# Mamba block, quantized MLP and mixture of experts on one core: the order of work at the hand-over between two batches

## The chip, the cores and the metric

The kernel runs on one core of one Trainium2 chip, as one launch. The metric is the device time of that launch in microseconds (us), the median of several runs. Engines are named as in the profile: PE is TensorE, DVE is VectorE, ACT is ScalarE, POOL is GpSimd, SP is SyncE, which here only issues DMAs.

## The reference

x has 4 batches of 512 tokens by 512 features. Each batch passes three layers, each with a layer norm ahead of it and added to x behind it:

- a Mamba mixer: `xi` and `z` (1024 channels each) by one projection; a causal convolution of 4 taps over xi and a silu give u; a projection of u gives dt (128), B and C (16 each); delta = softplus(dt_w dt + bias); a scan over time h = exp(delta A) h + delta u B for 1024 channels times 16 states, y = sum over the states of h C, plus u D; y silu(z), then an output projection;
- an MLP of two linears in simulated int8 (`_smooth_quant_linear`): columns of activations and weights are smoothed by their maxima, rows are scaled and rounded to integers, multiplied, and scaled back; a silu gate lies between the two, and the weights are the batch's own;
- a mixture of 16 experts, 2 for each token, and a shared expert.

## The kernel before

**Tiles and stages.** The channels lie in 8 blocks of 128 partitions, time in 512 columns. A unit is one block with one state: 128 units a batch. VectorE runs a scan and a product with C for each unit. A chunk, on GpSimd, is delta u B for two units (`chunk`, L665, one operation on 128x1024). ScalarE makes the exponentials of delta A (`decay`), and TensorE adds up the products of the states with identity matmuls.

The program is a row of stages: `first`, then for each batch b a `scan_stage(b)`. In the scan stage of batch b the experts of batch b-1 run beside the scan. Between two scan stages stands `between(a, m)` with a = m+1, the hand-over: the projections, convolution, dt, B, C and delta of batch a, woven by hand with the quantized MLP of batch m. There are three of these (a = 1, 2, 3). `last` does the MLP of the last batch alone. Every engine has its own instruction list, written out by hand in this order; they meet by semaphores only, and each engine runs strictly in its order.

**The hand-over on TensorE** (L2144 to L2193). xi and z blocks are eight matmuls each, dl (L1894) is one block of delta. The second MLP layer (layer 1) is `gated_rows` (transposes of the gated activations, L2095), `diag_rows` (broadcasts the smoothing factors along rows, L2057), `scale_rows` (the weights' scales, L2066), `integers` (transposes, L2072), and `linear` (L2086). Before the change `gated_rows` stands behind z2 and dl 1, and `linear(m, 1)` behind z6 and dl 5.

**On ScalarE** (L1136 to L1190): `gates` (L1109) is the silu of layer 0's output, `relus` (L901) gives the abs and the relu of delta's input, `exps` and `lns` the other parts of the softplus, `magic_rows` (L1082) the rounding, `weight_scales` (L1099) the copy of the scales, `row_norm` (L1091) the norm ahead of the experts. `decay` for the first three units stands behind the last z copy and ahead of the second `row_norm`.

**On VectorE** (L1580 to L1638): the class `Quant` has the MLP's steps; `one_more` and `lost` (L1276, L1288) are the softplus steps on e = exp(-|x|) of one block: w = e + 1, then e is overwritten by what the rounding of w lost. Blocks 0 to 3 stand inside layer 1's steps, blocks 4 to 7 behind `row_stats` and directly ahead of the scan.

**On GpSimd** (L699 to L716, L785 to L823): `softplus_sum` adds the logarithm to delta, `softplus_less` subtracts what was lost, then `du_block` and the chunks. The scan stage's loop runs over k, one chunk for each k; `pair` adds two products.

**Where e lies.** `sp_e` (L261) puts e of blocks 0 to 3 in `pairs` and of blocks 4 to 7 in `work[:, 4096:6144]`. The same columns of `work` are slots 2 and 3 of the four chunk slots (`dBu`, L220), so `chunk` waits for the subtractions of two blocks each before chunks 2 and 3:

```python
                if k in (2, 3) and b > 0:
                    pool.wait_ge(S["delta_ready"], NBLK * b + 2 * k + 2)
```

CB, the tile of C's rows broadcast over the partitions, has rows 12 to 15 that the MLP uses as scratch in the hand-over: `dg` (the diagonals) in rows 12 and 13, `wsc` (the copy of the scales) in row 14, `wrow` in row 15 (L235, L236, L252).

**Loads.** SyncE runs one list (L559 to L599). z's and xi's weights go through a ring of four slots (`wst`, `weight`, L398); a load waits until the block four places earlier is done. `bc_rows` writes B and C to DRAM, `broadcast(b, g)` (L436) reads four rows of B and four of C back, 1 MB each, for all partitions: group 0 once the first layer's integers are made, group 1 after the second linear, groups 2 and 3 after its residual, each with loads between them. ScalarE's queue stores the last batch's output (1 MB, L938) from a = 2 on. GpSimd's scan loop, ScalarE's x copies for the router (`x3`, L969, which wait for all eight sums because x3T holds the w of blocks 4 to 7), the logits (L1929), the router on VectorE and the first expert (L1971) follow in the first steps of the scan stage.

## Time and profile before

| | us |
|---|---|
| median of 3 runs | 1658.12 |
| lowest and highest | 1655.14, 1658.79 |
| the profiled execution, its time | 1660.13 |
| its span, first to last instruction | 1658.4 |
| its mean granted TensorE clock, of full speed | 0.937 |

The profiled execution is 2.0 us above the median; 1.7 us of its time lie outside the span. Times in the views are us from the start of the span. In a timeline several equal operations are merged into one row with their count; the bracket is the idle time of the engine ahead of the row and what ended it. Busy matmul times are modelled at their ends, so a chain of z blocks takes 3.44 us a block although a row says 3.60, and a delta block 0.86 although it says 1.02 or 1.10.

### The profile page before, as it was taken

Reading aid. Unit: us, or ns where it says so; the run is one execution under the profiler, and the core shown is the slowest. Engines: PE = TensorE matmul, PEld = TensorE weight load, DVE = VectorE, ACT = ScalarE, POOL = GpSimd, SP = SyncE. Lnnn points to the kernel's source line nnn. Section 1 sums busy time; section 2 is a strip of 40 time slices with the busy share of each in tenths; the row PEclk is TensorE's granted clock in tenths of the full one; section 3 lists DMA queues with packets and bytes.
Section 4 is the critical chain, followed back from the end, with each engine's and each line's share of the span. In section 5 each row is a group of like instructions: output and inputs, shape, how many; then the busy total and the mean of one; then the engine's idle time right before and its main releaser. Section 6 shows DMA issues by size and latency. Waiting matters only on the chain.

```text
span 1658.4 us, 19268 instructions
## 1 busy us (share of the span) xinstructions
PE 1415.7 (85%) x5374; PEld 811.2 (49%) x5382; DVE 1321.6 (80%) x2196; ACT 802.4 (48%) x1369; POOL 1033.5 (62%) x672
## 2 busy tenths in 40 slices
PE   7588678997799899998799899998699899646994
PEld 4333234443465565444465565444456564334783
DVE  4588999687899999696899999786899999774212
ACT  3675444247445765337444765347544654131131
POOL 0399899104899898303899898403999898422001
PEclk9799889999799999999799999999799999868997
DMA  3550000414346683504446673604445773601984
GB/s 120 223 190 25 1 0 31 141 32 183 134 153 217 211 246 111 187 26 177 161 146 223 213 238 104 206 26 156 182 147 183 219 240 103 240 25 43 351 327 136
DMA packets 94073, 252.13 MB, mean 152 GB/s; under 512 B 11024, under 2 KB 11152, under 8 KB 88848
## 3 DMA queue, kind: packets, MB, share of 16 engines
q1 hardware_dynamic: 86688, 229.93, 40.9%
q0 software_dynamic: 5120, 16.78, 3.0%
q10 hardware_dynamic: 2160, 4.19, 0.8%
q8 instruction: 44, 0.72, 0.2%
q14 instruction: 61, 0.50, 0.1%
HBM read 207.87 MB, written 42.99 MB: 151 GB/s over the span
## 4 chain that ended last, share of the span: by engine, by line
PE 45%; DVE 20%; issue 14%; POOL 13%; ACT 4%; DMA 3%; DVEq 0%; POOLq 0%; SPq 0%; ACTq 0%
PE bank L1991 10%; POOL work L674 6%; DVE bank L1306 5%; PE bank L1831 5%; PE bank L2117 5%; PE bank L1921 4%; PE bank L1926 4%; PE bank L2020 3%; PE bank L1915 2%; PE bank L1844 2%; PE bank L2012 2%; DVE pairs L1316 2%; PE bank L1967 2%; DVE work L1316 1%; DMA wst<-in_w_in 1%
## 5 line engine op out<-in xcount | busy, mean ns | idle before, releaser
L674 POOL TENSOR_TENSOR work<-du,BB 128x1024 f32<-128x1024 f32 x255 | 599.1, 2357 | 5.4 <-DVE work L1577 3.5
L962 ACT ACTIVATE bank<-delta,A_sb 128x512 f32<-128x512 f32 x512 | 349.2, 690 | 450.7 <-DVE pairs L1316 242.3
L1306 DVE TENSOR_TENSOR_SCAN bank<-bank,work 128x512 f32<-128x512 f32 x432 | 522.0, 1220 | 27.3 <-POOL work L674 21.1
L1991 PEld LDWEIGHTS bank<-x3T,ew_up 128*128 128x128 f32 x1488 | 217.9, 193 | 73.7 <-issue 63.7
L1991 PE MATMUL bank<-x3T,ew_up 128*128 128x128 f32 (+1 forms) x1488 | 239.7, 306 | 2.2 <-issue 2.2
L1316 DVE TENSOR_TENSOR pairs<-bank,CB 128x512 f32<-128x512 f32 x240 | 161.7, 674 | 4.7 <-PE bank L1926 2.9
L1921 PE MATMUL bank<-pairs,ident 128*128 128x512 f32 x160 | 90.4, 649 | 47.0 <-POOL pairs L727 18.4
L1316 DVE TENSOR_TENSOR work<-bank,CB 128x512 f32<-128x512 f32 x192 | 128.9, 671 | 0.0
L624 POOL TENSOR_TENSOR col<-col,halfpow 128x4 f32<-128x4 f32 (+1 forms) x8 | 7.3, 912 | 191.4 <-DVE col L1454 191.4
L1844 PE MATMUL bank<-xT,wst 128*128 128x512 f32 x256 | 120.4, 617 | 4.6 <-DMA wst<-in_w_in 4.6
L2117 PE MATMUL bank<-wst,zg 128*128 128x512 f32 x256 | 117.0, 593 | 0.8 <-DVE zg L1326 0.8
L1831 PE MATMUL bank<-xT,wst 128*128 128x512 f32 x256 | 114.4, 593 | 0.7 <-ACT xT L843 0.7
L1333 DVE SCALAR_TENSOR_TENSOR etm<-etm,bank 128x128 f32<-128x128 f32 (+1 forms) x124 | 38.8, 313 | 85.8 <-ACT etm L1019 85.8
L1270 DVE SCALAR_TENSOR_TENSOR u<-etm,cw,u 128x512 f32<-128x512 f32 x96 | 71.9, 752 | 34.3 <-ACT u L863 31.9
L1921 PE MATMUL bank<-work,ident 128*128 128x512 f32 x160 | 85.2, 615 | 13.5 <-POOL work L727 10.0
L1926 PE MATMUL bank<-pairs,ident 128*128 128x512 f32 x160 | 89.0, 640 | 0.0
L727 POOL TENSOR_TENSOR work<-work,CB 128x512 f32<-128x512 f32 x64 | 81.3, 1270 | 11.1 <-DVE work L1306 11.0
L724 POOL TENSOR_TENSOR work<-work 128x512 f32<-128x512 f32 x48 | 60.7, 1265 | 43.2 <-DVE work L1316 43.2
L2020 PE MATMUL bank<-ew_dn,etm 128*128 128x512 f32 x138 | 72.2, 605 | 17.6 <-ACT x3T L1033 17.2
L1926 PE MATMUL bank<-work,ident 128*128 128x512 f32 x160 | 83.0, 600 | 0.0
L1844 PEld LDWEIGHTS bank<-xT,wst 128*128 128x128 f32 x256 | 50.2, 199 | 65.8 <-issue 64.5
L1306 DVE TENSOR_TENSOR_SCAN work<-bank,work 128x512 f32<-128x512 f32 x64 | 77.7, 1214 | 4.6 <-ACT bank L962 2.4
(263 smaller groups left out, 2364.5 us busy)
## 6 DMA issues: line engine op xcount, KB each, us to landing
ew_up<-in_exp_w SPq DMA_DIRECT2D x93, 512.0 KB, 3.8
ew_dn<-in_exp_w SPq DMA_DIRECT2D x93, 256.0 KB, 4.3
hm<-xs_dram SPq DMA_DIRECT2D x69, 256.0 KB, 4.6
ys_dram<-x3T SPq DMA_DIRECT2D x69, 256.0 KB, 4.3
wst<-in_w_in SPq DMA_DIRECT2D x64, 256.0 KB, 2.7
BB<-bc_dram SPq DMA_DIRECT2D x16, 1024.0 KB, 7.3
CB<-bc_dram SPq DMA_DIRECT2D x16, 1024.0 KB, 9.8
wst<-in_out_w SPq DMA_DIRECT2D x32, 256.0 KB, 3.0
```

Source lines behind the costliest of these rows:

```text
L674: nc.gpsimd.tensor_tensor(dBu[:, k % CHUNK_SLOTS, :, :], du[:, j % 2:j % 2 + 1, :].broadcast_to([P, 2, T]), BB[:, n0:n0 + 2, :], ALU.mult) ...
L727: nc.gpsimd.tensor_tensor(hi, hi, CB[:, (2 * m + 1) % NS, :], ALU.mult).then_inc(S["pool_prod"], 1)
L962: nc.scalar.activation(R[q % RING][:, :], delta[:, j, :], ACT.Exp, scale=A_sb[:, j, n:n + 1]).then_inc(S["da_ready"], 1)
L1306: V.tensor_tensor_scan(prod[c % (2 * PAIR_SLOTS)] if on_pool(q) else R[q % RING][:, :], R[q % RING][:, :], dBu[:, c // 2 % CHUNK_SLOTS, c ...
L1316: V.tensor_tensor(prod[c % (2 * PAIR_SLOTS)], R[q % RING][:, :], CB[:, n, :], ALU.mult).then_inc(S["prod_done"], 1)
L1831: ins = mm(ps[:, :], wst[:, slot, k * P:(k + 1) * P], xT[:, k, :], start=(k == 0), stop=(k == KD - 1))
L1844: ins = mm(z_bank(a, m)[:, :], wst[:, slot, k * P:(k + 1) * P], xT[:, k, :], start=(k == 0), stop=(k == KD - 1))
L1921: mm(Y[:, :], ident[:], prod[2 * (m % PAIR_SLOTS)], start=(m % (NS // 2) == 0), stop=False)
L1926: mm(Y[:, :], ident[:], prod[2 * (m % PAIR_SLOTS) + 1], start=False, stop=(m % (NS // 2) == NS // 2 - 1)).then_inc(S["nsum_done"], 1)
L1991: ins = mm(gu_bank(v)[:, part * n:(part + 1) * n], w[:, part * D + k * P:part * D + (k + 1) * P], rhs, start=(k == 0), stop=(k == KD - 1))
L2020: mm(down_ps[1][:, :], eT[:, v % 2, 0:P], w, start=True, stop=True).then_inc(S["down_done"], 1)
L2117: ins = mm(acc[t][:, :], zg[:, k, t * P:(t + 1) * P], wst[:, W_POS["o", m, k] % W_RING, :], start=(k == 0), stop=(k == NBLK - 1))
```

## The change

- `sp_e`: e of blocks 4 to 7 lies in CB rows 13, 15, 12 and 14 instead of `work`. ScalarE's abs of these blocks gets waits until the diagonals, the scales and the second layer's scaling are done with these rows.
- C rows 12 to 15 are broadcast last, on a semaphore of their own (`c_last`), when all subtractions are done and the first expert loads are issued; what reads C's last four rows waits for that. GpSimd's chunks wait only for B's rows of group 3.
- Chunks 2 and 3 lose their wait. In the loop, chunk 2 stands ahead of the four sums of blocks 4 to 7 and chunk 3 ahead of their four subtractions.
- SyncE loads z weights 4 and 5 ahead of B and C's way through DRAM.
- ScalarE: `gates` ahead of block 0's abs and relu; the roundings, the scale copy and block 4's abs and relu each moved up.
- VectorE: `one_more` and `lost` of blocks 0 to 3 are spread one by one over layer 1's steps.
- TensorE: `gated_rows` directly behind dl 0, the diagonals behind z2, the scales and integers behind z4 and dl 3, the second linear behind dl 4; z5, z6 and dl 5 follow it.

```diff
-            return pairs[:, m, :] if m < 4 else work[:, 4096 + (m - 4) * T:4096 + (m - 3) * T]
+            return pairs[:, m, :] if m < 4 else CB[:, (13, 15, 12, 14)[m - 4], :]
...
+        def b_rows_in(eng, b, n):
+            eng.wait_ge(bcast[n // 4], (16 if n >= 12 else 32) * (b + 1))
+
+        def c_rows_in(eng, b, n):
+            if n >= 12:
+                eng.wait_ge(S["c_last"], 16 * (b + 1))
+            else:
+                eng.wait_ge(bcast[n // 4], 32 * (b + 1))
...
+            def broadcast(b, g, half):
+
+                dst, landed = ((BB, bcast[g]), (CB, S["c_last"] if g == 3 else bcast[g]))[half]
+                if b > 0 and g == 3 and half == 1:
+                    sp.wait_ge(S["delta_ready"], NBLK * (b + 1))
...
                 weights("z", b, 0, 4)
+                if b > 0:
+                    weights("z", b, 4, 6)
                 bc_rows(b)
 
                 if b > 0:
                     wait(sp, "q_ready", 4 * TT * (b - 1) + 2 * TT)
-                    broadcast(b, 0)
-                    weights("z", b, 4, NBLK)
+                    broadcasts(b, 0)
+                    weights("z", b, 6, NBLK)
                     wait(sp, "lin_ps", 2 * TT * b)
-                    broadcast(b, 1)
+                    broadcasts(b, 1)
                     weights("o", b, 0, 4)
                     wait(sp, "linkO", 3 * TT * b)
-                    broadcast(b, 2)
-                    broadcast(b, 3)
+                    broadcasts(b, 2)
+                    broadcast(b, 3, 0)
                     load_first_experts(b - 1)
+                    broadcast(b, 3, 1)
                     load_experts(b - 1)
...
-                if k in (2, 3) and b > 0:
-                    pool.wait_ge(S["delta_ready"], NBLK * b + 2 * k + 2)
...
+                        if k > (1 if b > 0 else 0):
+                            chunk(b, k)
                         if k == 2 and b > 0:
                             for i in range(4, 8):
                                 softplus_sum(b, i)
-                            for i in range(4, 6):
-                                softplus_less(b, i)
-                        if k > (1 if b > 0 else 0):
-                            chunk(b, k)
-                        if k == 2 and b > 0:
-                            for i in range(6, 8):
+                        if k == 3 and b > 0:
+                            for i in range(4, 8):
                                 softplus_less(b, i)
...
+                    elif m == 4:
+                        sc.wait_ge(S["sbc_ps"], 2 * (2 * a - 1) + 1)
+                    elif m == 6:
+                        sc.wait_ge(S["wsc_ps"], 2 * a)
+                    elif m == 7:
+                        sc.wait_ge(S["linkO"], 3 * TT * (a - 1) + 2 * TT)
...
+                gates(m)
                 relus(a, range(0, 1))
-                gates(m)
...
                 exps(a, range(1, 2))
+                magic_rows(m, 1, 0)
                 z(a, 3)
                 relus(a, range(2, 3))
                 exps(a, range(2, 3))
-                magic_rows(m, 1, 0)
+                magic_rows(m, 1, 1)
                 z(a, 4)
                 relus(a, range(3, 4))
+                weight_scales(m, 1)
                 exps(a, range(3, 4))
-                magic_rows(m, 1, 1)
                 lns(a, range(4))
-                weight_scales(m, 1)
+                relus(a, range(4, 5))
                 z(a, 5)
-                relus(a, range(4, 5))
+                relus(a, range(5, 6))
                 z(a, 6)
-                relus(a, range(5, 8))
+                relus(a, range(6, 8))
...
-                for i in range(2):
-                    one_more(a, i)
-                    lost(a, i)
+                one_more(a, 0)
+                lost(a, 0)
                 q1.scale(0)
                 q1.maxima(0)
+                one_more(a, 1)
+                lost(a, 1)
                 q1.scale(1)
                 q1.maxima(1)
                 q1.weight_diag()
-                for i in range(2, 4):
-                    one_more(a, i)
                 q1.integers(0)
-                for i in range(2, 4):
-                    lost(a, i)
+                one_more(a, 2)
+                lost(a, 2)
                 q1.integers(1)
+                one_more(a, 3)
+                lost(a, 3)
...
                 dl(a, 0)
+                gated_rows(m)
                 z(a, 2)
+                diag_rows(m, 1, 0)
+                diag_rows(m, 1, 1)
                 dl(a, 1)
-                gated_rows(m)
                 z(a, 3)
                 dl(a, 2)
-                diag_rows(m, 1, 0)
-                diag_rows(m, 1, 1)
                 z(a, 4)
                 dl(a, 3)
-                z(a, 5)
-                dl(a, 4)
                 scale_rows(m, 1)
-                z(a, 6)
                 integers(m, 1, 0)
                 integers(m, 1, 1)
+                dl(a, 4)
+                linear(m, 1)
+                z(a, 5)
                 dl(a, 5)
-                linear(m, 1)
+                z(a, 6)
                 dl(a, 6)
                 dl(a, 7)
                 z(a, 7)
```

## Rows read from the trace of the kernel before

**Rows 1.** The page, busy us, share of the span, instructions.

```profile
PE 1415.7 (85%) x5374; PEld 811.2 (49%) x5382; DVE 1321.6 (80%) x2196; ACT 802.4 (48%) x1369; POOL 1033.5 (62%) x672
```

**Rows 2.** Windows: length; busy PE, PEld, DVE, ACT, POOL; granted clock; DMA share; GB/s.

```profile
420.00:440.00 20.00, 12.67 (x31) 6.19 (x32) 13.59 (x17) 9.55 (x17) 19.66 (x13) 0.66 0.32 127
...
560.00:580.00 20.00, 19.25 (x99) 12.80 (x97) 19.98 (x31) 14.47 (x27) 20.00 (x12) 1.00 0.76 224
```

**Rows 3.** Timeline of TensorE, second hand-over: start, us, operation, [idle before <-releaser].

```profile
746.71 1.10 PE L1902 MATMUL bank<-hm,dtw 128*128 128x512 f32 x2 [0.76 <-ACT hm L894]
...
760.31 5.37 PE L1844 MATMUL bank<-xT,wst 128*128 128x512 f32 x8 [2.15 <-DMA wst<-in_w_in]
...
777.21 1.67 PE L2091 MATMUL bank<-CB 128*128 128x512 bf16 x7 [0.25 <-DVE CB L1514]
...
780.44 3.60 PE L1844 MATMUL bank<-xT,wst 128*128 128x512 f32 x8
...
800.23 6.33 PE L1932 MATMUL bank<-x3T,gatew 128*17 128x512 f32 x8 [7.03 <-ACT x3T L980]
...
808.73 5.41 PE L1991 MATMUL bank<-x3T,ew_up 128*128 128x256 f32 x16
```

**Rows 4.** Timeline of VectorE, the same stretch.

```profile
753.01 1.29 DVE L1450 TENSOR_REDUCE col<-bank 128x1 f32<-128x512 f32 x2 [2.13 <-PE bank L2099]
...
756.71 0.42 DVE L1286 TENSOR_SCALAR work<-pairs 128x512 f32<-128x512 f32 x1
...
788.88 2.73 DVE L1294 SCALAR_TENSOR_TENSOR work<-x3T,work 128x512 f32<-128x512 f32 x1
...
792.59 2.34 DVE L1306 TENSOR_TENSOR_SCAN bank<-bank,work 128x512 f32<-128x512 f32 x2
...
803.56 1.23 DVE L1306 TENSOR_TENSOR_SCAN bank<-bank,work 128x512 f32<-128x512 f32 x1 [4.62 <-POOL work L674]
...
826.31 0.67 DVE L1316 TENSOR_TENSOR work<-bank,CB 128x512 f32<-128x512 f32 x1
```

**Rows 5.** Timeline of GpSimd, the same stretch.

```profile
788.52 2.54 POOL L674 TENSOR_TENSOR work<-du,BB 128x1024 f32<-128x1024 f32 x1
...
793.56 4.94 POOL L645 TENSOR_TENSOR delta<-delta,x3T 128x512 f32<-128x512 f32 x4 [2.50 <-ACT x3T L936]
...
809.60 2.35 POOL L674 TENSOR_TENSOR work<-du,BB 128x1024 f32<-128x1024 f32 x1
```

**Rows 6.** The chain that ended last, the same stretch: start, us, what.

```profile
749.12 11.06 DMA wst<-in_w_in
```

**Rows 7.** Timeline of ScalarE, the same stretch.

```profile
749.00 1.33 ACT L1112 ACTIVATE BB<-BB 128x256 f32<-128x256 f32 x4
...
788.60 2.94 ACT L1096 ACTIVATE xn<-x,row_shift,rstd 128x512 f32<-128x512 f32 x4 [0.41 <-POOL row_shift L636]
```

**Rows 8.** Timeline and window of VectorE alone: reciprocal of the weights; length, busy us.

```profile
765.06 0.18 DVE L1495 RECIPROCAL rr<-rr 128x4 f32<-128x4 f32 x1
...
756.71:771.65 14.94, 12.60 (x41) 0.89 0.26 101
```

**Rows 9.** SyncE's issues of B and C rows: us to landing.

```profile
DMA to landing us min/median/max: 4.2/8.9/18.8
```

**Rows 10.** Timeline of TensorE, third hand-over.

```profile
1183.85 5.41 PE L1991 MATMUL bank<-x3T,ew_up 128*128 128x256 f32 x16
```

**Rows 11.** Timelines of TensorE, ScalarE and GpSimd, first hand-over.

```profile
373.84 1.10 PE L1902 MATMUL bank<-hm,dtw 128*128 128x512 f32 x2 [0.76 <-ACT hm L894]
...
413.67 2.93 ACT L1096 ACTIVATE xn<-x,row_shift,rstd 128x512 f32<-128x512 f32 x4 [1.58 <-POOL row_shift L636]
...
433.79 5.34 PE L1991 MATMUL bank<-x3T,ew_up 128*128 128x256 f32 x16
...
434.66 2.35 POOL L674 TENSOR_TENSOR work<-du,BB 128x1024 f32<-128x1024 f32 x1
```

**Rows 12.** Window of TensorE: length, busy us, granted clock, DMA share, GB/s.

```profile
762.00:764.00 2.00, 2.00 (x4) 0.50 0.00 0
```

More of the change, by code:

```diff
@@ L328, in build @@
             "xi_ps xpad_ready conv_done u_ready z_ps z_ready bc_ps tok_ps tok_ready bc_ready bc_out dt_ps dt_ready dl_ps "
-            "sp_abs sp_exp relu_ready sp_w_ready sp_ln_ready sp_lost sum_ready z_silu delta_ready "
+            "sp_abs sp_exp relu_ready sp_w_ready sp_ln_ready sp_lost sum_ready z_silu c_last delta_ready "
             "a_shift_ready "
@@ L434, in bc_rows, with broadcasts @@
                 sp.wait_ge(S["bc_out"], 16 * b + 16)
-            def broadcast(b, g):
-                for half, dst in enumerate((BB, CB)):
-                    rows = bc_dram[half * NS + 4 * g:half * NS + 4 * g + 4, :]
-                    sp.dma_start(dst[:, 4 * g:4 * g + 4, :],
-                                 rows.rearrange("n t -> (n t)").partition_broadcast(P)
-                                 .rearrange("p (n t) -> p n t", n=4)).then_inc(bcast[g], 16)
+            def broadcast(b, g, half):
+                dst, landed = ((BB, bcast[g]), (CB, S["c_last"] if g == 3 else bcast[g]))[half]
+                if b > 0 and g == 3 and half == 1:
+                    sp.wait_ge(S["delta_ready"], NBLK * (b + 1))
+                rows = bc_dram[half * NS + 4 * g:half * NS + 4 * g + 4, :]
+                sp.dma_start(dst[:, 4 * g:4 * g + 4, :],
+                             rows.rearrange("n t -> (n t)").partition_broadcast(P)
+                             .rearrange("p (n t) -> p n t", n=4)).then_inc(landed, 16)
+            def broadcasts(b, g):
+                for half in range(2):
+                    broadcast(b, g, half)
             def expert(be, w):
@@ L580, in _ @@
                     for g in range(4):
-                        broadcast(b, g)
+                        broadcasts(b, g)
                     weights("z", b, 4, NBLK)
@@ L1311, in product @@
                     ve.wait_ge(S["scan_done"], q + 1)
-                    ve.wait_ge(bcast[n // 4], 32 * (b + 1))
+                    c_rows_in(ve, b, n)
                     wait(ve, "nsum_done", PAIRS * b + c // 2 - PAIR_SLOTS + 1)
```

4 lines of the change are left out of this document (2 added, 2 removed).

## The prediction

> **What bounds it now.** On the page TensorE is busy 85% of the span [rows 1], so the first question is where it is not. The busy time by 20 us shows it: well inside a scan stage (560 to 580) TensorE, VectorE and GpSimd are all busy 19 us or more of 20, while at the hand-over into that stage (420 to 440) TensorE has 12.7 us and a granted clock of 0.66, and VectorE 13.6 [rows 2]. There are three such hand-overs (a = 1, 2, 3), some 375 us apart; the change touches nothing else. I read the second, engine by engine, in the timelines.
>
> TensorE first [rows 3]. It stands 2.15 us for the DMA of z's block-4 weights, and that block then takes 5.37 us instead of 3.60: together 3.9 us. After its last z block it has nothing to do but the transposes of x, and starts the router's logits at 800.23 and the first expert at 808.73. VectorE [rows 4] waits 2.13 us for the gated rows' transposes, stands again ahead of the transposed integers, and waits 4.62 us in the scan for GpSimd. GpSimd [rows 5] is what VectorE waits for: chunk 1 at 788.52, then a hole, four sums at 793.56, then the subtractions mixed with chunks 2 and 3, because these chunks overwrite the e of blocks 4 to 7; chunk 4 ends at 809.60+2.35 = 811.95. The chain of waits agrees: DMA, TensorE, VectorE's second layer, the last softplus blocks, GpSimd.
>
> **The change, step by step (second hand-over, us).**
> 1. *z weights 4 and 5 earlier.* Now they are issued behind 2 MB of B and C rows, and z4's load takes 11.06 us [rows 6]. Ahead of those, with SyncE idle anyway, they are in long before use: the 2.15 and the 1.77 us of slow clock go. z6 and z7 stay behind the rows; they are needed 20 us after their issue, against those 11: no cost. The rows themselves leave at the same time.
> 2. *Gates before the block-0 softplus on ScalarE, gated rows before z2 on TensorE.* The gates start at 749.00 [rows 7] behind two operations of 0.68; now near 746.5. TensorE has the first delta block done at 747.65 [rows 3], idles some 0.6 us and ends the transposes at 748.6; the reduction starts at 748.7 instead of 753.01 [rows 4], 4.3 earlier. From there to the end of the diagonals are 3.7 us: 752.4.
> 3. *TensorE up to the second linear.* From 752.4: second row broadcast 0.5, two z blocks of 3.44, three delta blocks of 0.86, gives 762.4. VectorE has 12.6 us of work between the diagonals and the end of the integers [rows 8], the same instructions in another order, so it could be at 765.0. Later is ScalarE: the reciprocals of the weights' maxima come 8.5 us behind the diagonals as before (765.06+0.18 against 756.71 [rows 4, 8]), at 760.9; rounding, four operations, 2.1, 763.0; then z4's copy, abs and relu of block 3, the scale copy and the exponential, five operations on 128x512 of 0.5 to 0.6 net: 765.8. VectorE's one_more and lost of block 3 now stand ahead of both transposed copies, so these wait for that exponential: 1.1 plus 1.3 us, linear at 768.2. Before: 777.21 [rows 3], so 9.0 us earlier.
> 4. *What is late next.* z5, block 5, z6 (7.7 us) now follow the linear. It ends at 769.8, so blocks 6 and 7 start at 777.6 instead of 778.7: only 1.1 of the 9.0 us is left. From there ScalarE takes 9.5 us (abs and relu, table load, four exponentials, z7, three decays) to the row normalization at 788.60 less 0.41 of wait [rows 7]: 787.1. VectorE, early by 9, stands idle some 5 us before the exponentials of blocks 4 to 7.
> 5. *e in CB's last rows, chunks 2 and 3 ahead of the subtractions.* From row normalization to the first sum are 4.96 us [rows 5, 7]: 792.1. Chunk 2 falls into the hole before it, at no cost. Then four sums 4.94, chunk 3 2.35, four subtractions of the same length, a pair (one such operation, 1.25), chunk 4 2.35: 808.0 instead of 811.95, 3.95 earlier.
> 6. *VectorE's start of the scan.* One `lost` took 2.73 us instead of 0.69: it ran beside chunk 1 and ended 0.55 us behind it [rows 4, 5]. Now two chunks lie beside these operations instead of one, so I let two of them wait: from 783 the eight operations end at 791.0, against 792.59. Without any such wait it would be 787. The logits start 7.6 us behind the scan (800.23 against 792.59 [rows 3, 4]), because ScalarE's x copies stand behind a decay that waits for VectorE's third product: 798.6, one us later than the sums allow. Then 6.33 us, and 1.1 for a copy and the small transposes: first expert at 806.0 instead of 808.73, 2.7 earlier.
> The Trainium skill, GPSIMD Engine Reference, section Specifications, says that GpSimd's SBUF interfaces are shared with VectorE and contend with its instructions that have two SBUF inputs. The trace agrees: `lost` has two, and the scan's products, with one input in a bank, do not stretch. By that rule chunk 2 is not free: the sum without it would have the first expert 2 us earlier, and the 791.0 is the value with it.
> 7. *C rows 12 to 15 last.* They leave when the subtractions end, 804.4. A landing took 4.2 to 18.8 us, median 8.9 [rows 9]: 809 to 823. The product of unit 12 starts at 826.31 [rows 4], then near 823. Hidden. The waits that relu 4, 6 and 7 get are for things 5 us or more older. SyncE's wait in front of the third up weight holds nothing: that load waits for the first expert, at 806 plus.
>
> **Sum.** TensorE is 2.7 and GpSimd 3.95 us earlier, and the stage behind is bound by both: 3.3. The third hand-over is the same (first expert at 1183.85 [rows 10], 0.3 later in the pattern): 3.6. The first [rows 11] has no DMA wait. Its first delta block is at 373.84, so shifted by 372.9 us the row normalization would come at 414.2 against 413.67, later; first expert 433.1 against 433.79, chunk 4 at 435.1 against 437.01: 1.3. Together 8.2.
>
> One cost is open: TensorE's clock. Around the linear it stands 1.6 us for the scales, works 1.3, stands 1.6 again. A stand of 2.15 us brought the granted clock to 0.50 (1.2 GHz, the lower of its two levels) at 762 [rows 3, 12] and cost 1.77; one of 0.76 (ahead of 746.71 [rows 3]) left it at full speed. So between 0 and 1.8 us for each hand-over; two stands of 1.6 lie about as near the one as the other, so 0.9 for each: 2.7. The forecast is 8.2 - 2.7 = 5.5 us, from the profiled 1660.13 to 1654.6, and from the median of 1658.12, which is 2.0 lower, to 1652.6.
>
> **Rivals.**
> *More comes through.* All of VectorE's 4.6 and 1.4 us of waits in the early scan go, and the router is not last. For it: GpSimd, not TensorE, feeds the scan there. Against: the normalization still waits for z7's side. It gives 4 to 6 us for each, 12 to 18, some 1643. Chance 0.11.
> *Nothing measurable.* The tail of step 4 runs at the slow clock in all three, and `lost` waits for three GpSimd operations: 1.8 us later in each and another us from the port: 8.2 - 5.4 - 2 = 0.8, about 1657. For it: the first hand-over has no margin. Chance 0.20. 0.2% is 3.3 us, about what a measurement of this kernel can tell from no change.
> *Slower: the tail.* The same mechanism, one step more: TensorE has stood before the gated rows too (0.76 and 0.6 us), and if the clock is down from there, z2 ends 1.8 later, the diagonals and linear 1.4, and z5 with the next slow stretch 1.8: 3.2 against margins of 0.7, 2.7 and 3.0, and GpSimd beside it. It decides from a linear later than 770.9 in the second hand-over (2.7 us past my 768.2); at 773 in all three it costs 3 to 6 us: 1661 to 1664. Against: the idle of 0.76 ahead of the first delta block [rows 3] is followed by z blocks at full speed in all three hand-overs. Chance 0.14.
> *The C rows late* would need a landing of over 18 us on an empty queue: under 0.01. That the change does not do what it says is out for step 1, since the two loads have no other wait.
>
> **Numbers.** The forecast's own case (3.3 to 12 us faster) has 0.55; its range is 1646.5 to 1654.8. With the rivals: faster 0.66, same 0.20, slower 0.14. Leaving out most of the fast rival and half of the slow one, the range is 1646.5 to 1661.
>
> **What would show it.** Right: no DMA wait ahead of z4 and 3.6 us for it; gated rows' transposes ahead of z2; the linear near 768 in the pattern; VectorE idle some 5 us ahead of one_more of block 4; chunk 2 ahead of the sums; the scan's wait of 4.6 gone; the first expert 1, 3 and 3 us earlier. Wrong: a z5 of over 5 us at a clock of 0.50 in all three; a row normalization later than before in the second; a product waiting for C rows; or a scan stage that gives the start back, its length then more than before by the same us.

## The result and the profile after

The changed kernel takes 1648.43 us (median of 4 runs, 1647.67 to 1649.87) against 1658.45 us for the kernel before (4 runs): ratio 0.9934, 95% interval 0.9911 to 0.9956. It is 10.0 us faster; forecast were 5.5 us, with a range of 1646.5 to 1661. Its profiled execution took 1648.9 us, span 1647.2 us, which is 11.2 us less than the span of before (1658.4).

The page of the changed kernel (busy us, share of the span; for a line also count, mean ns, and the idle time ahead of it). The second and the third line are the scan on VectorE and the matmuls of the z blocks on TensorE.

```profile
PE 1411.3 (86%) x5382; PEld 809.1 (49%) x5382; DVE 1327.2 (81%) x2196; ACT 802.4 (49%) x1369; POOL 1033.4 (63%) x672
...
L1328 DVE TENSOR_TENSOR_SCAN bank<-bank,work 128x512 f32<-128x512 f32 x432 | 522.3, 1221 | 13.7 <-POOL work L691 7.4
...
L1867 PE MATMUL bank<-xT,wst 128*128 128x512 f32 x256 | 116.2, 599 | 0.0
```

The same two lines of the page of the kernel before:

```profile
L1306 DVE TENSOR_TENSOR_SCAN bank<-bank,work 128x512 f32<-128x512 f32 x432 | 522.0, 1220 | 27.3 <-POOL work L674 21.1
...
L1844 PE MATMUL bank<-xT,wst 128*128 128x512 f32 x256 | 120.4, 617 | 4.6 <-DMA wst<-in_w_in 4.6
```

The work is that of [rows 1], within 6 us on every engine; what went is waiting. The idle time ahead of these scans fell from 27.3 to 13.7 us, that for GpSimd from 21.1 to 7.4, and no z block waits for a DMA any more.

Busy time in windows of the changed kernel (columns as in [rows 2]): the first hand-over, and the same piece of a scan stage.

```profile
420.00:440.00 20.00, 13.16 (x40) 6.52 (x41) 17.02 (x34) 10.67 (x19) 20.00 (x15) 0.75 0.45 162
560.00:580.00 20.00, 19.25 (x95) 12.56 (x95) 18.15 (x26) 12.97 (x24) 19.47 (x12) 1.00 0.74 223
```

VectorE has 17.0 us of 20 instead of 13.6 at the hand-over, and TensorE's granted clock is 0.75 instead of 0.66. The scan stage's window shows less on VectorE (18.2 against 20.0); its cause comes below.

TensorE's timeline at the second hand-over of the changed kernel. Its first delta block starts at 745.94, where it was 746.71 before [rows 3], so 0.77 us go off a time of before ahead of a comparison.

```profile
745.94 1.10 PE L1925 MATMUL bank<-hm,dtw 128*128 128x512 f32 x2 [0.76 <-ACT hm L909]
746.87 1.20 PE L2122 MATMUL bank<-ident,BB 128*128 128x128 f32 x8
747.91 3.60 PE L1867 MATMUL bank<-xT,wst 128*128 128x512 f32 x8
...
764.61 0.62 PE L2104 MATMUL bank<-identb,BB 128*128 128x128 bf16 x8 [1.12 <-ACT CB L1122]
765.06 1.08 PE L1925 MATMUL bank<-hm,dtw 128*128 128x512 f32 x2
767.52 1.90 PE L2114 MATMUL bank<-CB 128*128 128x512 bf16 x8 [1.38 <-DVE CB L1536]
769.26 3.60 PE L1867 MATMUL bank<-xT,wst 128*128 128x512 f32 x8
...
798.54 5.41 PE L1955 MATMUL bank<-x3T,gatew 128*17 128x512 f32 x8 [7.57 <-ACT x3T L1001]
804.62 0.42 PE L1959 MATMUL bank<-ident,hm 17*128 17x17 f32 x4 [0.67 <-ACT hm L1007]
804.97 3.72 PE L2014 MATMUL bank<-x3T,ew_up 128*128 128x256 f32 x16
808.52 1.02 PE L1938 MATMUL bank<-pairs,ident 128*128 128x512 f32 x2
```

The gated rows' transposes stand ahead of z2, the second linear starts at 767.52, and the z block behind its two stands of 1.12 and 1.38 us runs at full speed. The first expert takes 3.72 us where it took 5.41 [rows 3]. Nothing in the forecast was a price for that. Both levels of the clock are in these rows: the granted clock is 0.50 in the first 2 us of the logits (798.5 to 800.5), and full in the whole expert.

Granted clock around that expert, of the kernel before and then of the changed one (length, busy us of PE, PEld, DVE, ACT, POOL, granted clock, DMA share, GB/s):

```profile
806.00:808.00 2.00, 0.56 (x2) 0.00 (x0) 1.09 (x2) 0.97 (x3) 1.93 (x1) 1.00 0.00 0
808.00:810.00 2.00, 1.62 (x8) 1.39 (x9) 1.48 (x2) 0.32 (x1) 2.00 (x3) 0.79 0.00 0
810.00:812.00 2.00, 2.00 (x6) 1.55 (x6) 2.00 (x4) 0.69 (x1) 2.00 (x2) 0.50 0.03 8
```

```profile
802.00:804.00 2.00, 1.95 (x5) 0.28 (x3) 2.00 (x3) 0.01 (x1) 2.00 (x3) 0.95 0.00 0
804.00:806.00 2.00, 1.38 (x9) 1.25 (x10) 0.56 (x3) 2.00 (x4) 2.00 (x2) 1.00 0.78 254
```

Before, the clock came back in the logits and fell to 0.50 (1.2 GHz) again behind a stand of TensorE of 1.82 us. In the changed kernel that stand is 0.67 us, and the clock stays at 1.00 (2.4 GHz).

VectorE and GpSimd of the changed kernel, same stretch:

```profile
748.11 1.29 DVE L1472 TENSOR_REDUCE col<-bank 128x1 f32<-128x512 f32 x2 [0.53 <-PE bank L2122]
...
782.44 0.43 DVE L1308 TENSOR_SCALAR x3T<-CB 128x512 f32<-128x512 f32 x1 [5.21 <-ACT CB L941]
782.90 2.73 DVE L1316 SCALAR_TENSOR_TENSOR CB<-x3T,CB 128x512 f32<-128x512 f32 x1
785.55 2.57 DVE L1308 TENSOR_SCALAR x3T<-CB 128x512 f32<-128x512 f32 x1
...
790.89 2.34 DVE L1328 TENSOR_TENSOR_SCAN bank<-bank,work 128x512 f32<-128x512 f32 x2
...
807.11 2.35 DVE L1328 TENSOR_TENSOR_SCAN bank<-bank,work 128x512 f32<-128x512 f32 x2 [1.55 <-POOL work L691]
```

```profile
782.50 5.33 POOL L691 TENSOR_TENSOR work<-du,BB 128x1024 f32<-128x1024 f32 x2
791.32 4.93 POOL L664 TENSOR_TENSOR delta<-delta,x3T 128x512 f32<-128x512 f32 x4 [3.49 <-ACT x3T L957]
...
804.64 2.36 POOL L691 TENSOR_TENSOR work<-du,BB 128x1024 f32<-128x1024 f32 x1
```

VectorE idles 5.21 us for an exponential of ScalarE, as forecast; two of its operations, a `lost` and a one_more, are stretched beside chunks 1 and 2. The scan's wait of 4.62 us [rows 4] is now one of 1.55, for chunk 4.

To compare kernels, the table gives starts in the second hand-over in us behind the first delta block, from the timelines, and as forecast (its times less 746.71). Below, a time with a + is such a time.

| | before | forecast | changed |
|---|---|---|---|
| second linear | 30.50 | 21.5 | 21.58 |
| row normalization | 41.89 | 40.4 | 40.44 |
| scan | 45.88 | 44.3 | 44.95 |
| chunk 4 | 62.9 | 58.9 | 58.7 |
| logits | 53.52 | 51.9 | 52.60 |
| first expert (its length) | 62.02 (5.41) | 59.3 | 59.03 (3.72) |
| first state sum | 67.26 | | 62.58 |

The row of the second linear of before shows 7 of its 8 matmuls, so its real start is about 0.2 us earlier; the same holds below where the linear reads +21.8, which is the 21.58 of the changed kernel.

The last row is 2.40, 4.68 and 4.94 us earlier at the three hand-overs, together 12.0. VectorE's gated products (y times silu(z), one for each block), taken from the last one of a stage to the first of the next, are earlier by the same 2.4, 4.65 and 4.9. The sum of the three shifts of these gated products is called the hand-over gain below.

### The profile page after: what moved, and what is told of

It is laid out like the page before. It is cut to its first block, busy times and chain, and to the rows that moved or that the text cites. A ratio compares the mean times of both kernels' runs of the same rounds, so it can differ in the third digit from the quotient of the medians.

```text
span 1647.2 us, 19279 instructions
## 1 busy us (share of the span) xinstructions
PE 1411.3 (86%) x5382; PEld 809.1 (49%) x5382; DVE 1327.2 (81%) x2196; ACT 802.4 (49%) x1369; POOL 1033.4 (63%) x672
## 4 chain that ended last, share of the span: by engine, by line
PE 47%; DVE 22%; issue 12%; POOL 10%; ACT 5%; DMA 2%; DVEq 0%; SPq 0%; POOLq 0%; ACTq 0%
PE bank L2014 10%; DVE bank L1328 5%; POOL work L691 5%; PE bank L1854 5%; PE bank L2140 5%; PE bank L1944 4%; PE bank L1949 4%; PE bank L2043 4%; PE bank L1938 3%; PE bank L1867 2%; PE bank L2035 2%; PE bank L1990 2%; DVE pairs L1338 2%; DVE work L1338 1%; DVE rr L1512 1%
## 5 line engine op out<-in xcount | busy, mean ns | idle before, releaser
L1328 DVE TENSOR_TENSOR_SCAN bank<-bank,work 128x512 f32<-128x512 f32 x432 | 522.3, 1221 | 13.7 <-POOL work L691 7.4
L2014 PEld LDWEIGHTS bank<-x3T,ew_up 128*128 128x128 f32 x1488 | 218.6, 195 | 74.5 <-issue 65.7
L1867 PE MATMUL bank<-xT,wst 128*128 128x512 f32 x256 | 116.2, 599 | 0.0
L1854 PE MATMUL bank<-xT,wst 128*128 128x512 f32 x256 | 114.4, 593 | 0.7 <-ACT xT L858 0.7
L1867 PEld LDWEIGHTS bank<-xT,wst 128*128 128x128 f32 x256 | 49.3, 194 | 60.3 <-issue 58.7
```

The costliest lines, as they stand in the source:

```text
L1328: V.tensor_tensor_scan(prod[c % (2 * PAIR_SLOTS)] if on_pool(q) else R[q % RING][:, :], R[q % RING][:, :], dBu[:, c // 2 % CHUNK_SLOTS, c ...
L1854: ins = mm(ps[:, :], wst[:, slot, k * P:(k + 1) * P], xT[:, k, :], start=(k == 0), stop=(k == KD - 1))
L1867: ins = mm(z_bank(a, m)[:, :], wst[:, slot, k * P:(k + 1) * P], xT[:, k, :], start=(k == 0), stop=(k == KD - 1))
L2014: ins = mm(gu_bank(v)[:, part * n:(part + 1) * n], w[:, part * D + k * P:part * D + (k + 1) * P], rhs, start=(k == 0), stop=(k == KD - 1))
```

## The experiments

The theory after the result (A): the hand-over gain is the order's (rows, scales and the second linear earlier) together with the C part's (e in CB's last rows, so that chunks 2 and 3 need not wait: GpSimd's hole filled, chunk 4 earlier), and TensorE's first expert comes out at the higher clock. Rival B: one part alone does it, the z weights above all. The first four kernels ran on one chip, beside 31 runs of before (median 1659.05 us).

**The z weights alone** (`w_only`): the kernel before with

```diff
+                if b > 0:
+                    weights("z", b, 4, 6)
...
-                    weights("z", b, 4, NBLK)
+                    weights("z", b, 6, NBLK)
```

> The kernel before with one part of the change alone: z weights 4 and 5 loaded ahead of the B and C rows. Theory A (the gain is made of three parts, each of which only lets the next one act): the second and third hand-over then look like the first one of the kernel before, whose first expert comes 2.1 and 2.4 us earlier in the pattern, so about 4.5 us faster in all, 1654; z4 takes 3.60 us with no wait in all three. Theory B (the DMA wait with its slow clock, 3.9 and 4.2 us, was nearly all of it and passes through whole): 8 us faster, about 1650. Theory C (hidden anyway): 1658.

Measured: 1657.65 us (12 runs, one of which took 3360.13 us and is not in the ratio), ratio 0.9986 [0.9967, 1.0005]. The z wait goes, but the scan starts at +43.6 in all three hand-overs where it was +43.6, +45.9 and +46.2, so that two of them gain about 2 us; the first expert took 5.3, 3.72 and 6.74 us. The hand-over gain is 0, 3.3 and 0.8 us. The early weights alone give less than a measurement can tell: the interval leaves room for the 4.5 us of theory A, not for the 8 us of theory B, so the weights were not nearly all of it.

**The orders undone** (`order_undone`): the changed kernel with the three engines' orders of before; on TensorE

```diff
-                gated_rows(m)
                 z(a, 2)
-                diag_rows(m, 1, 0)
-                diag_rows(m, 1, 1)
                 dl(a, 1)
+                gated_rows(m)
...
-                dl(a, 4)
-                linear(m, 1)
                 z(a, 5)
...
+                linear(m, 1)
```

> The changed kernel with the orders of TensorE, ScalarE and VectorE as before (gated rows behind z2, second linear behind z6); the early z weights, e in CB's rows and chunks 2 and 3 ahead of the subtractions stay. Theory A: chunk 2 fills GpSimd's hole, so chunk 4 ends some 2.4 us earlier than in the kernel with the weights alone, but the linear stays late; about 1651 to 1653, the first expert 1 to 2 us later than in the changed kernel. Theory B: the same as the changed kernel, 1648.5.

Measured: 1656.15 us (12 runs), ratio 0.9978 [0.9958, 0.9999].

**The C part undone** (`c_undone`): the changed kernel with the e of blocks 4 to 7 in the chunks' buffers again, so that chunks 2 and 3 wait for the subtractions, and C's last rows loaded with B's:

```diff
-            return pairs[:, m, :] if m < 4 else CB[:, (13, 15, 12, 14)[m - 4], :]
+            return pairs[:, m, :] if m < 4 else work[:, 4096 + (m - 4) * T:4096 + (m - 3) * T]
...
+                if k in (2, 3) and b > 0:
+                    pool.wait_ge(S["delta_ready"], NBLK * b + 2 * k + 2)
```

> The changed kernel without the part on e and the chunks (e of blocks 4 to 7 in work, C rows with the B rows, chunks 2 and 3 behind the subtractions as before); early z weights and the new orders stay. Theory A: VectorE waits for GpSimd ahead of unit 4 again (4 to 5 us), chunk 4 ends 2.4 us later than in the changed kernel, while only one lost operation is stretched; about 1651 to 1653. Theory B: the same as the changed kernel, 1648.5.

Measured: 1657.68 us (12 runs), ratio 0.9987 [0.9966, 1.0009]. The expectations (1651 to 1653 for both) missed: a third and a fifth of the changed kernel's gain are left in the medians, where more than half was expected; the hand-over gains are 5.5 and 2.4 us of 12.0. With `w_only` these runs make a square: the hand-over gain is 4.1 us with the early weights alone (ratio 0.9986), 2.4 with the orders added (0.9987), 5.5 with the C part added (0.9978), and 12.0 with both (0.9934). Each part adds little or nothing without the other, which also excludes rival B. The timelines say why. In `order_undone` the logits start at +54.4 instead of +52.6 and the first expert at +61.3 to +61.8: the scan is late. In `c_undone` the logits start earlier than in the changed kernel (+52.0), and yet the first expert comes at +60.5 to +60.7. VectorE, ScalarE and TensorE of `c_undone`, second hand-over:

```profile
803.43 1.23 DVE L1309 TENSOR_TENSOR_SCAN bank<-bank,work 128x512 f32<-128x512 f32 x1 [4.66 <-POOL work L676]
```

```profile
805.28 0.69 ACT L964 ACTIVATE bank<-delta,A_sb 128x512 f32<-128x512 f32 x1 [3.81 <-DVE pairs L1319]
807.00 0.69 ACT L964 ACTIVATE bank<-delta,A_sb 128x512 f32<-128x512 f32 x1 [1.02 <-DVE work L1319]
807.62 0.57 ACT L988 COPY hm<-bank 17x512 f32<-17x512 f32 x1
```

```profile
808.25 0.51 PE L1940 MATMUL bank<-ident,hm 17*128 17x17 f32 x4 [2.14 <-ACT hm L988]
```

The scan waits for GpSimd; ScalarE's decays wait for the scan's products; the copy of the logits is queued behind two of them on ScalarE; TensorE stands 2.14 us for it (2.41 and 2.77 at the other two hand-overs), and its expert then takes 6.63, 5.25 or 3.72 us in the three hand-overs. With the C part there is no such wait: in every kernel that has it, above and below, TensorE's stand is 0.66 to 0.67 us and the expert takes 3.72 us at all three. So the second order and the C part are not two gains that add; the scan's start and GpSimd's chunks each hold the other's gain back.

**The z weights undone** (`w_undone`): the changed kernel with the first diff reversed.

> The changed kernel with z weights 4 and 5 behind the first B and C rows again. Theory A: z4 is now due at 757.7 in the second hand-over and waits 2 to 3 us for its weights there and in the third, with a slow clock behind it, so the linear is 4 us later in these two: 5 to 8 us slower than the changed kernel, 1654 to 1656. If VectorE's and ScalarE's own chain (the exponential of block 3) hides the wait, 1650.

Measured: 1648.24 us (8 runs), ratio 0.9929 [0.9905, 0.9952], like the changed kernel. TensorE of `w_undone`, second hand-over:

```profile
755.22 1.95 PE L1865 MATMUL bank<-xT,wst 128*128 128x512 f32 x4 [0.39 <-DMA wst<-in_w_in]
```

This view ends in the middle of the block. The wait is 0.39 us there and 1.82 at the third hand-over, and the whole z block of eight matmuls takes 3.67 us behind either, so neither is followed by a slow one. The second linear is at +21.80, +21.82 and +23.25; the hand-over gain is 2.4, 5.8 and 3.8, together 12.0. The expected 1654 to 1656 were wrong; the alternative that the expectation named, a wait hidden by the chain of VectorE and ScalarE, is what the second hand-over shows, while at the third the linear is 1.5 us late. In the new order the weights' lead is worth nothing that shows in the medians.

The next four ran on a second chip (before: 1659.52 us, 11 runs). **Chunk 2 behind the sums** (`chunk2_late`):

```diff
                     if k > (1 if b > 0 else 0) and not (k == 2 and b > 0):
                         chunk(b, k)
                     if k == 2 and b > 0:
                         for i in range(4, 8):
                             softplus_sum(b, i)
+                        chunk(b, k)
```

> The changed kernel with one thing put back: GpSimd's chunk 2 of a block stands again behind the four sums of the softplus, not ahead of them; the C rows stay in CB's last rows. Theory A (the hole of GpSimd before the sums is what the C part gives): chunk 2 beside VectorE's last softplus operations is gone, so these take about 0.7 instead of 2.6 to 2.7 us and the scan starts about 2 us earlier (+42.8 instead of +44.95 us behind the first transpose of the gated rows' stage), but chunk 4 starts at about +61.1 instead of +58.7, the scan waits some 4.7 us for chunk 3 as in the run with the C part undone, ScalarE's exponential behind it keeps the router's copy back, and the first expert comes at about +60.6: about 1656 us, ratio 0.997 to 0.999, nearly all of the gain gone. Theory B (the two stretched operations of VectorE are a real cost and the hole is worth little): the scan's earlier start comes through, about 1646 us or less, ratio at or below 0.992.

Measured: 1654.22 us (5 runs), ratio 0.9966 [0.9952, 0.998]. VectorE of `chunk2_late`, second hand-over:

```profile
783.57 2.73 DVE L1317 SCALAR_TENSOR_TENSOR CB<-x3T,CB 128x512 f32<-128x512 f32 x1
786.22 0.41 DVE L1309 TENSOR_SCALAR x3T<-CB 128x512 f32<-128x512 f32 x1
...
810.07 2.35 DVE L1329 TENSOR_TENSOR_SCAN bank<-bank,work 128x512 f32<-128x512 f32 x2 [3.39 <-POOL work L691]
```

The one_more is back at 0.41 us, and the scan starts at +42.8 instead of +44.95: chunk 2 beside VectorE costs 2.2 us, as the sum's step 6 had it. But chunk 4 starts at +61.0 instead of +58.7 and the scan waits 3.39 us for it. The first expert comes at +58.9, no later than in the changed kernel (+60.6 had been expected), and still the hand-over gain is only 7.3 us instead of 12.0. So GpSimd's chunk 4 binds beside TensorE: its 2.3 us at each of three hand-overs cost 4.7 us of the hand-over gain, and 5 us between the two ratios to the kernel before. Theory A had the binding engine right and the first expert wrong.

**Scales and normalization early** (`norm_early`): VectorE's stand of 5.21 us says what to move next. On TensorE, with ScalarE in the same order:

```diff
                 dl(a, 4)
+                dl(a, 5)
                 linear(m, 1)
                 z(a, 5)
-                dl(a, 5)
-                z(a, 6)
                 dl(a, 6)
                 dl(a, 7)
+                z(a, 6)
                 z(a, 7)
```

and on GpSimd `norm(2 * m + 1)` ahead of the sum of block 3 instead of behind it.

> The changed kernel with the softplus chain moved up once more: the inputs of the scales of blocks 5 and 7 on TensorE ahead of the second linear and of z6, the rectified blocks and exponentials of ScalarE in the same order, and GpSimd's row normalization ahead of its sum of block 3. Theory A (the chain of the scales on ScalarE and VectorE sets when the scan starts, since VectorE stood 5.21 us for an exponential): the scan and x3 start 2 to 3 us earlier at each of three hand-overs, TensorE's stand of 7.57 us ahead of the logits falls to about 5, and the time is about 1641 to 1643 us, ratio about 0.989. Theory B (chunk 4 of GpSimd and TensorE's first expert bind, not the start of the scan): the earlier start is given back at chunk 4 (the scan waited 1.55 us for it already), within 2 us of the changed kernel: 1646 to 1649 us, ratio 0.992 to 0.994.

Measured: 1640.53 us (4 runs), ratio 0.9886 [0.9869, 0.9904]. VectorE of `norm_early`:

```profile
772.17 0.69 DVE L1307 TENSOR_SCALAR x3T<-CB 128x512 f32<-128x512 f32 x1 [0.92 <-ACT CB L941]
```

The stand is 0.92 us, the scan starts at +40.8, the logits at +49.6, the first expert at +56.0, +57.0 and +55.6. The hand-over gain against before is 21.3 us.

**The clock kept up** (`warm`): the changed kernel with dummy products, 28 behind the transposes of x and, once the second residual is done, 20 behind z7:

```diff
+                    if scan:
+                        for i in range(28):
+                            mm(Y[:, 0:P], ident[:], ones[:], start=True, stop=True)
...
+                pe.wait_ge(S["linkO"], 3 * TT * (m + 1))
+                for i in range(20):
+                    mm(acc[0][:, 0:P], ident[:], ones[:], start=True, stop=True)
```

> The changed kernel with dummy products of the identity and a 128x128 tile of ones, whose results nobody reads: 20 behind z7 and 28 behind the transposes of x, in TensorE's stands of 5.0 and 7.6 us. Theory A (the granted clock of 1.2 GHz in the logits is a cost on the path): the logits take about 3.5 instead of 5.4 us, the first expert and the first state sum come about 1.5 to 2 us earlier at each of three hand-overs, about 1643 to 1645 us, ratio 0.990 to 0.992. Theory B (chunk 4 and the scan of VectorE bind there as well, 1.55 us of wait for chunk 4): the logits are shorter in the trace, but VectorE's later products come at the same time and the time is that of the changed kernel, 1647 to 1649 us, ratio 0.993 to 0.994.

Measured: 1644.08 us (6 runs), ratio 0.9911 [0.9892, 0.993]. TensorE of `warm`, first and second hand-over:

```profile
426.94 5.30 PE L1955 MATMUL bank<-x3T,gatew 128*17 128x512 f32 x8 [2.30 <-ACT x3T L1001]
...
796.40 3.61 PE L1955 MATMUL bank<-x3T,gatew 128*17 128x512 f32 x8 [2.30 <-ACT x3T L1001]
```

The stand ahead of the logits is 2.30 us at all three, and the logits took 5.30, 3.61 and 5.19 us: the clock was kept in one of three (granted clock 1.00 through its logits, 0.62 and 0.50 in the first 2 us of the others). There the first state sum is 1.8 us earlier, and 0.3 and 0.2 in the others. The hand-over gain of this profile is 14.3 us, 2.3 more than the changed kernel's. The interval overlaps that of the changed kernel, so this points to A and doesn't prove it.

**Both** (`warm_norm`), with 14 and 20 dummies:

> Both edits of the two runs before together, with 14 and 20 dummy products. If the chain of the scales and the clock of the logits are two costs one behind the other, their gains add: about 1637 to 1640 us, ratio 0.987 to 0.989. If GpSimd's chunk 4 binds behind either, it is no better than the better of the two, ratio 0.990 to 0.994.

Measured: 1642.87 us (4 runs), ratio 0.9895 [0.9878, 0.9912]: no better than `norm_early`. The stand ahead of the logits is 3.47 us, and they took 5.3, 6.35 and 4.9 us, as in `norm_early` without the dummies, so with these counts they kept no clock, and whether the two gains would add stays open.

The last four, on a third chip (before: 1658.65 us, 11 runs). **The changed kernel once more** (`changed_again`):

> The changed kernel itself once more, beside the others on one chip. Theory A (its fall of the granted clock in the scan stage, 0.70 and 0.50 where other kernels show 1.00 behind the same stands, and the 1.8 us that it costs at two of three hand-overs, is a property of this order of instructions): the two falls are there again in the trace, ratio 0.993. Theory B (it is chance from one execution to the next): the stretch between the second and fourth gated block of a stage shows 1.00, the last mixer row of TensorE comes some 2 to 4 us earlier than 1423.6 us, and the ratio is between 0.990 and 0.994.

Measured: 1648.76 us (5 runs), ratio 0.994 [0.9926, 0.9954]: the gain is there again. The hand-over gain is 12.5 us against 12.0, in the three hand-overs 0.65, 5.6 and 6.2 against 2.4, 4.65 and 4.9, so one hand-over of one profile can be off by 1.7 us while the sum holds. Where the clock falls in the scan stages is read in the next section.

**Scales early without the edit on GpSimd** (`scales_early`):

> The run with the earlier softplus chain without its edit on GpSimd: TensorE and ScalarE take the scales' blocks 5 and 7 earlier, GpSimd's row normalization stays behind its sums and differences of block 3. Theory A (ScalarE's last exponentials alone set when VectorE's second half of the softplus begins): VectorE goes on 2 to 3 us earlier, at +34 instead of +36.5 us, but the row normalization, which x3 waits for, stays at about +40.4, so that x3 and the logits come as in the changed kernel (+52.6) and chunk 2 starts as late (+36.5): about 1646 us, ratio 0.991 to 0.993. Theory B (the earlier normalization is not needed): as in the run with both, 1640.5 us, ratio 0.989.

Measured: 1640.65 us (4 runs), ratio 0.9891 [0.9876, 0.9905], and the row normalization at +38.05 as in `norm_early`. The expectation had missed that it stands behind the same exponentials on ScalarE; GpSimd's edit is worth nothing that shows. This, a swap on TensorE and ScalarE alone, is the version to keep: 8 us faster than the changed kernel on the same chip.

**The first pair sum behind chunk 4** (`norm_pair`): `norm_early` with

```diff
-                        pair(k - PAIR_BEHIND)
+                        if not (b > 0 and k == PAIR_BEHIND):
+                            if b > 0 and k == PAIR_BEHIND + 1:
+                                pair(0)
+                            pair(k - PAIR_BEHIND)
```

> The best kernel so far (scales and normalization early) with one more exchange on GpSimd: the first pair sum of a block, 1.27 us, behind chunk 4 instead of ahead of it. The scan waited 1.22 us for chunk 4 there, and TensorE reads the pair sum only after the first expert, 4 us later. Theory A (GpSimd's chunk 4 binds VectorE's scan at each of three hand-overs, and TensorE is not the bound): the wait is gone, the later products come up to 1.2 us earlier each, 1637 to 1639 us, ratio 0.987 to 0.988. Theory B (TensorE's first state sum at +59.1 to +60.5 us behind the first transpose binds): no change, 1640.5 us, ratio 0.988 to 0.990.

Measured: 1644.25 us (5 runs), ratio 0.9908 [0.9894, 0.9922]. VectorE's next product, in `norm_early` and then in `norm_pair`:

```profile
798.77 2.34 DVE L1327 TENSOR_TENSOR_SCAN bank<-bank,work 128x512 f32<-128x512 f32 x2 [1.22 <-POOL work L691]
801.67 0.69 DVE L1337 TENSOR_TENSOR pairs<-bank,CB 128x512 f32<-128x512 f32 x1 [0.56 <-PE bank L1937]
```

```profile
800.00 2.35 DVE L1330 TENSOR_TENSOR_SCAN bank<-bank,work 128x512 f32<-128x512 f32 x2
804.11 0.69 DVE L1340 TENSOR_TENSOR pairs<-bank,CB 128x512 f32<-128x512 f32 x1 [1.76 <-PE bank L1940]
```

The wait for GpSimd is gone, and the same 1.2 us stand one row on, for TensorE's first state sum, which is where it was. In that order TensorE's first expert binds. Down to the last mixer row (TensorE's last output projection of the scan stages) the profile is that of `scales_early` (1413.86 against 1413.92 us); the 4.7 us between the spans of these two profiles lie in the last stage, and the two intervals overlap.

**The best kernel without early z weights** (`norm_no_w`):

> The best kernel so far without the early z weights: the 4th and 5th pair of z weights ordered behind the B and C rows again, as before the change. In the changed kernel taking them back cost nothing measurable (0.9929 against 0.9934), since the chain of the scales hid TensorE's wait. Theory A (here this chain is shorter by some 2.4 us, so the wait of z4, 0.4 to 1.8 us there, comes through): 1 to 4 us over the three hand-overs, ratio 0.990 to 0.992. Theory B (it is hidden still): ratio 0.988 to 0.989.

Measured: 1643.78 us (6 runs), ratio 0.991 [0.9894, 0.9926]. TensorE of `norm_no_w`, third hand-over:

```profile
1121.89 5.37 PE L1864 MATMUL bank<-xT,wst 128*128 128x512 f32 x8 [2.27 <-DMA wst<-in_w_in]
```

Here the wait is there with its slow z block, as in [rows 3], and the linear comes at +25.4 instead of +21.8, the scan at +44.4 instead of +40.8. At the first two hand-overs nothing changes. The hand-over gain is 16.3 us against 21.3 of `norm_early`. In the shorter order the weights' lead is worth up to 3.6 us for one hand-over in which the load is late; the medians point the same way, with intervals that overlap.

## Why the prediction was right, and what it mis-sized

Steps 1 to 7 were made in the times of before; set against the changed trace (the table above), they hold within 0.7 us.

*Steps 2 and 3.* The reduction starts 2.17 us behind the first delta block (forecast 2.0), the linear at 21.58 (21.5), after stands of 1.12 and 1.38 us. *Step 4.* Blocks 6 and 7 at +31.05 (30.9), row normalization at +40.44 (40.4): of 8.9 us at the linear, 1.45 are left. *Step 5.* The sums at +45.4 (45.4), chunk 4 done at +61.1 (61.3). *Step 6.* The scan at +44.95, 0.65 later than forecast; two operations were stretched as the step said, by 2.0 and 2.1 us: a `lost`, which has two inputs, and a one_more, which has one and went from 0.42 to 2.57 us. The Trainium skill, GPSIMD Engine Reference, section Specifications, gives the contention for VectorE's instructions with two SBUF inputs, which the prediction quoted, and also for those in a 2-port perf mode. The trace agrees for `lost`; no run here shows in which mode the one_more ran. The first expert came within 0.3 us of the forecast by luck in part: the scan was 0.65 late, and the logits took 5.41 us instead of the 6.33 taken over from before. *Step 7.* The C rows are issued at 803.50, and no product waits for them. The first hand-over has its first expert at +59.17 (forecast 433.1 less 373.84, so 59.3).

Four terms of the sum were off.

*The clock's cost, 2.7 us, was 0.* The two stands of about 1.6 us behind each other were 1.12 and 1.38, with 1.5 us of work between, and z5 took 3.60 us at all three hand-overs.

*The first expert's length was no term.* The sum counted its start (2.7 us for the second) and let its length stand. It went from 5.34, 5.41 and 5.41 us to 3.72, because the C part takes the decays' wait from ahead of the logits' copy. 5.0 us in all, and TensorE binds there beside GpSimd, whose chunk 4 is 2.1, 4.2 and 4.5 us earlier, so they come through: 2.3, 4.4 and 4.7 us by the forecast's starts with this length, 2.4, 4.7 and 4.9 measured. That the length comes through is seen in `c_undone`, whose first experts start within 0.2 us of each other: with 6.63, 5.25 and 3.72 us, the first state sum is at +67.2, +65.7 and +64.1. This is the step that failed, in its size: step 6 counted the shorter way from the logits to the expert (1.1 us instead of 2.2) and not what this does to the clock behind it.

*Step 1's 3.9 us* went into the sum only through what follows, and rightly small: `w_undone` shows nothing of it in the median in this order. In the trace of before, its wait and slow block came at two hand-overs of three; alone it is worth at most what `w_only` shows.

*The stages behind were taken as fixed.* Of the 12.0 us, 10.0 are in the medians. In the changed kernel's profile 1.8 us are given back in each of two scan stages, the second and the third: from the third to the fourth gated product it is 33.85 and 33.87 us, where it was 32.02 and 32.03 before. VectorE's wait for this is the 1.85 us missing in the window of 560 to 580 above. The windows, second scan stage of the changed kernel and then the same of `changed_again`:

```profile
548.00:552.00 4.00, 3.42 (x14) 2.49 (x14) 4.00 (x6) 3.23 (x6) 4.00 (x3) 0.70 0.74 248
552.00:556.00 4.00, 3.40 (x10) 2.31 (x10) 4.00 (x8) 2.34 (x5) 4.00 (x3) 0.50 0.22 81
```

```profile
548.00:552.00 4.00, 2.38 (x14) 1.74 (x14) 4.00 (x7) 3.24 (x5) 4.00 (x3) 1.00 0.78 260
552.00:556.00 4.00, 3.84 (x17) 2.38 (x18) 4.00 (x7) 2.27 (x5) 4.00 (x3) 1.00 0.24 74
```

Same kernel, same stand of 1.9 us ahead of it (548.58, for ScalarE), clock fallen in one execution and not in the other; in the third scan stage it fell in both. So the order alone does not fix it. But it fell in three of the four second and third scan stages of this kernel's two profiles, and in none of the 24 of the other twelve profiles, where the same stretch takes 32.0 to 32.1 us, `w_undone` with the same order among them. Whether this kernel makes the fall likelier or it is chance stays open. It is the part of the forecast's "give the start back" that did occur. The last stage, whose code is the same in all, took 223 to 230 us from the last mixer row to the end in these fourteen profiles (227.0 before, 223.6 in the changed kernel), which is why the span fell by 11.2 while the last mixer row came only 7.8 us earlier. So a few us between the spans of two single profiles say nothing here; medians and the whole hand-over gain do.

The forecast's own case gave 3.3 to 12 us, and its range began at 1646.5 us, which is 11.6 below the median of before; the measured 10.0 us are inside either, and nearly twice the 5.5 forecast.

*The rivals.* "More comes through" was right that the scan's wait of 4.6 us goes and that GpSimd feeds it, and `norm_early` shows the rest of its gain to be there: the stand of 5.21 us that step 4 named was worth another 8 us. "Nothing measurable" and "Slower: the tail" both needed the clock to fall around the linear. In none of the profiles with this order is a z block behind the linear slow; the one slow z block ahead of it, in `norm_no_w`, stands behind a wait for its weights.

## What to carry to other kernels

Ask of each change not only when an operation starts but at which clock it will run: the length of a matmul group behind a removed stand is a term of its own, here 5 of 12 us. When two engines bind the next stage together, undoing either part loses most of the gain, so single-part trials undervalue both. And read where an engine idles after the change: VectorE's 5.21 us for one exponential pointed at a swap of two blocks that gave 8 us more than the change had.

## What was not expected of the hardware

Single stalls with no cause in the profile. In `changed_again` one operation on 128x4 elements held VectorE for 7.25 us, where the kernel's four such operations take 0.34 us on average in the changed kernel's profile:

```profile
926.51 7.25 DVE L1274 SCALAR_TENSOR_TENSOR shift<-mv,rstd 128x4 f32<-128x4 f32 x1
```

Together with the fall of the clock at 920 it set the gated products back by 7.0 us against the kernel before (8.8 us early ahead of it, 1.8 behind). Nothing waits in the rows of the other engines that would explain it; its cause stays open.

A one-input operation of VectorE is stretched beside a GpSimd chunk as much as a two-input one (2.57 and 2.73 us), and ends 0.3 us behind the chunk, the two-input one of `chunk2_late` 0.6 behind. The one_more at 782.44, which began 0.06 us ahead of the chunk, took its usual 0.43 us.

And behind the same stand of TensorE the clock falls or holds: behind 1.9 us in the second scan stage it fell in one execution of the changed kernel and held in the other; behind 2.30 us in `warm` it held at one hand-over of three; and in `w_only` and `c_undone` the expert took 3.72 us behind the longest of the three stands (2.50 and 2.77 us) and 5.25 to 6.74 behind the shorter ones. Behind the 0.67 us ahead of the first expert it never fell.
